# One-hot matrices of a routing built row by row, the order of a kernel's set-up, and attention's maxima as two bf16 halves

## The reference

```python
x = x + moe_top2(layernorm(x), ctx)      # 8 experts, 128 -> 512 -> 128, relu; routed by the context
x = x + moe_top4(layernorm(x))           # 16 experts in 4 groups, the best 2 groups, 4 experts of them
x = x + attention(layernorm(x), ctx)     # 16 heads of 8, mask, softmax, output projection
x = x + 0.5 * mlp(layernorm(x))          # 128 -> 512 -> 128, silu, dequantised weights

# routing of the first layer
scores_topk, idx_topk = jax.lax.top_k(einsum(context, Wg) + bg, 2)
# routing of the second
masked = jnp.where(group_mask[:, :, None], g, -jnp.inf).reshape(T, E)
_, idx = jax.lax.top_k(masked, TOPK)
# softmax of the third
scores = jnp.where(mask, -jnp.inf, einsum('bhsd,bhtd->bhst', qh, kh) * scale)
probs = jax.nn.softmax(scores, axis=-1)
```

## Time and profile before

| | |
|---|---|
| time, median of 3 runs | 1053.17 us (1051.47 to 1054.09) |
| time of the profiled execution | 1050.84 us |
| its span, first to last instruction | 1049.0 us |
| PE busy | 811.3 us (77%) |
| DVE busy | 636.2 us (61%) |
| ACT busy | 500.6 us (48%) |
| POOL busy | 395.2 us (38%) |
| granted TensorE clock, mean | 0.876 of full |

### The profile page before, as it was taken

One profiled execution on the slowest core, in us unless ns is written; L12 is line 12 of the kernel. 1 busy time (PEld: TensorE's weight loads), 2 busy tenths in 40 slices (PEclk: granted clock), 3 DMA queues, 4 the chain that ended last, 5 costly groups with the idle time before them and its releaser, 6 DMA issues.

```text
span 1049.0 us, 17575 instructions
## 1 busy us (share of the span) xinstructions
PE 811.3 (77%) x5374; PEld 621.0 (59%) x5374; DVE 636.2 (61%) x1897; ACT 500.6 (48%) x984; POOL 395.2 (38%) x462
## 2 busy tenths in 40 slices
PE   6577187885789843769877566799789999989898
PEld 4475176764678733657666455688455555555575
DVE  5766053443555812557695344586778888887596
ACT  4443043442465422347644234476255555546586
POOL 5435733005510073443104545410466644446200
PEclk9589678898898965978988868799899999999899
DMA  8482246454311221171021131110344544543011
GB/s 286 132 269 92 87 116 196 164 200 145 103 49 39 71 67 27 42 282 41 23 66 44 53 102 42 57 29 22 105 129 133 139 119 118 165 114 107 5 31 50
DMA packets 96368, 106.54 MB, mean 102 GB/s; under 512 B 12604, under 2 KB 70348, under 8 KB 94999
## 3 DMA queue, kind: packets, MB, share of 16 engines
q1 hardware_dynamic: 76856, 78.04, 23.8%
q0 software_dynamic: 8608, 18.22, 6.8%
q10 hardware_dynamic: 10816, 9.16, 2.8%
HBM read 69.19 MB, written 36.18 MB: 100 GB/s over the span
## 4 chain that ended last, share of the span: by engine, by line
PE 50%; another core or an unknown queue 13%; issue 12%; DVE 11%; ACT 7%; POOL 3%; ACTq 1%; DMA 1%; SPq 1%; DVEq 0%; POOLq 0%
PE y_ps L1872 4%; PE y_ps L2094 3%; PE y_ps L1999 3%; PE hid_ps L1984 3%; PE hid_ps L1860 2%; PE hid_ps L2070 2%; PE hid_ps L2071 2%; PE hid_ps L2082 2%; PE hid_ps L1968 2%; PE tr_ps L2149 2%; PE hid_ps L1850 2%; PE tr_ps L2121 1%; PE hid_ps L1852 1%; PE hid_ps L1969 1%
## 5 line engine op out<-in xcount | busy, mean ns | idle before, releaser
L639 POOL DMA_INDIRECT xr<-b_tokens,idx_sb x70 | 67.0, 957 | 152.6 <-DVE idx_sb L899 105.7
L1121 DVE TENSOR_TENSOR hl<-hid_ps,hh 128x512 fp32r<-128x512 f32 x78 | 53.8, 690 | 110.7 <-ACT hh L1530 73.6
L1872 PE MATMUL y_ps<-region,hh 128*128 x312 | 91.8, 371 | 27.9 <-DVE hl L1121 16.6
L647 POOL DMA_INDIRECT yg<-a_rows,idx_a x64 | 60.9, 952 | 91.8 <-DMA a_rows<-yo 63.3
L1302 DVE TENSOR_REDUCE negmax<-hid_ps 128x4 f32<-128x512 f32 x128 | 85.8, 684 | 8.9 <-PE hid_ps L2071 7.9
L1872 PEld LDWEIGHTS y_ps<-region,hh 128*128 128x128 f32 x312 | 64.8, 208 | 37.0 <-issue 36.6
L1984 PE MATMUL hid_ps<-ident,zb 128*128 128x128 f32 x280 | 49.5, 306 | 45.9 <-DVE hl L1252 24.2
L1860 PE MATMUL hid_ps<-ident,zb 128*128 128x128 f32 x312 | 53.7, 301 | 38.8 <-issue 24.3
L1524 ACT ACTIVATE zb<-hid_ps 128x512 f32<-128x512 f32 x78 | 46.6, 597 | 77.1 <-PE hid_ps L1852 38.8
L1999 PE MATMUL y_ps<-region,hh 128*128 x280 | 82.1, 369 | 0.1
L1241 DVE TENSOR_TENSOR zb<-hid_ps,sg 128x256 f32<-128x256 f32 x70 | 29.7, 424 | 85.5 <-ACT sg L1626 51.3
(11 more groups left out here) (354 smaller groups left out, 2365.1 us busy)
## 6 DMA issues: line engine op xcount, KB each, us to landing
region<-k_strips SPq DMA_DIRECT2D x128, 64.0 KB
region<-k_strips SPq DMA_DIRECT2D x32, 256.0 KB
region<-hl SPq DMA_DIRECT2D x128, 64.0 KB
k_strips<-k_halves SPq DMA_DIRECT2D x24, 256.0 KB
region<-nought SPq DMA_DIRECT2D x6, 1024.0 KB
a_rows<-yo SPq DMA_DIRECT2D x20, 256.0 KB
b_rows<-yo SPq DMA_DIRECT2D x18, 256.0 KB
staged<-a_w_in SPq DMA_DIRECT2D x16, 256.0 KB, 5.8
```

What stands on the lines that cost most here:

```text
L639: g.indirect_dma_start(xr[:, q % 3, j * RB:j * RB + w], None, src, bass.IndirectOffsetOnAxis(ap=rows.bitcast(U32), axis=0)).then_inc(x_got ...
L647: g.indirect_dma_start(yg[:, b % 2, k, j * P:(j + 1) * P], None, ys[h], bass.IndirectOffsetOnAxis(ap=idx[:, h, k, t:t + 1].bitcast(U32), a ...
L1121: v.tensor_tensor(hl[:, n % 2, :], hid_ps[2 + n % 2][:], hh[:, n % 2, :].bitcast(F32), ALU.subtract).then_inc(a_hl, 1)
L1872: t.matmul(y[:, c0:c0 + 2 * P], hh[:, n % 2, cs], w2a[:, bass.ds(e * (2 * FA) + c * 2 * P, 2 * P)], start=c == 0, stop=False)
```

## The change

Three edits.

1. `tile_hots` and `row_hots` make each column of tokens (16 or 2 x 16) in an instruction of its own, tensor_scalar, which compares with a value per partition and, in tile_hots, multiplies with a second one. The operands lohi and idf become fp32; the 0..127 row and the matrices stay fp16.
2. In the set-up ACT copies and rounds only 4 of the 8 folded parts before the tables and the other 4 behind them; PE's prefix sums stand behind the fourth fold instead of the eighth; the wait for the bias row stands behind ACT's first copy.
3. nmpad becomes a bf16 tile at another place of the same memory; DVE writes the high half of the maxima straight into it and the low half by a subtraction that reads it; nm16 and its copy go. PE transposes it with plain bf16 matmuls against a bf16 identity.

```diff
-        id16 = sb("id16", [P, TH], F16)
-        lohi16 = sb("lohi16", [P, 4 * TH], F16)
+        idf = sb("idf", [P, TH])
+        lohi = sb("lohi", [P, 4 * TH])
...
-        nmpad = cpad[:, BT:2 * BT].rearrange("p (b h r) -> p b h r", b=NT, h=HG)
+        nmpad = brows[:, 2 * BT:3 * BT].rearrange("p (b h r) -> p b h r", b=NT, h=HG)
...
             def tile_hots(n, buf):
                 hot = buf[:, 0:2 * TH * n].rearrange("p (k n) -> p k n", k=2 * TH)
-                link(v.tensor_tensor(hot, spread(io16[:], [0, 2 * TH], [1, n]), spread(lohi16[:, 2 * TH:], [1, 2 * TH], [0, n]),
-                                     ALU.is_equal))
-                hot4 = buf[:, 0:2 * TH * n].rearrange("p (k t n) -> p k t n", k=2, t=TH)
-                v.tensor_tensor(hot4, hot4, spread(id16[:], [0, 2], [1, TH], [0, n]), ALU.mult).then_inc(hots, 1)
+                for k in range(2 * TH):
+                    ins = v.tensor_scalar(hot[:, k, :], io16[:, 0:n], lohi[:, 2 * TH + k:2 * TH + k + 1], idf[:, k % TH:k % TH + 1],
+                                          ALU.is_equal, ALU.mult)
+                ins.then_inc(hots, 1)
 
             def row_hots(c, buf):
-                v.tensor_tensor(buf.rearrange("p (k r) -> p k r", r=P), spread(io16[:], [0, TH], [1, P]),
-                                spread(lohi16[:, c * TH:], [1, TH], [0, P]), ALU.is_equal).then_inc(hots, 1)
+                rows = buf.rearrange("p (k r) -> p k r", r=P)
+                for t in range(TH):
+                    ins = v.tensor_scalar(rows[:, t, :], io16[:], lohi[:, c * TH + t:c * TH + t + 1], None, ALU.is_equal)
+                ins.then_inc(hots, 1)
...
-                link(v.tensor_copy(nm16[:, s % 2], negmax[:, s % 2]))
-                v.tensor_copy(nmpad[:, :, :, 3 * HD], nm16[:, s % 2])
-                v.tensor_tensor(nmpad[:, :, :, 3 * HD + 1], negmax[:, s % 2], nm16[:, s % 2], ALU.subtract).then_inc(c_nm, 1)
+                link(v.tensor_copy(nmpad[:, :, :, 3 * HD], negmax[:, s % 2]))
+                v.tensor_tensor(nmpad[:, :, :, 3 * HD + 1], negmax[:, s % 2], nmpad[:, :, :, 3 * HD], ALU.subtract).then_inc(c_nm, 1)
...
-            eng.wait_ge(in_last, 16)
-            for k in range(EA):
+            def unfold(k):
                 eng.wait_ge(fold_mm, k + 1)
                 a.activation(fold_buf(k)[0:P - 1, :], hid_ps[k % 4][0:P - 1, :], ACT.Copy).then_inc(folded, 1)
                 eng.wait_ge(folded, k + 1)
+                if k == 0:
+                    eng.wait_ge(in_last, 16)
                 split_high(k)
+
+            for k in range(EA // 2):
+                unfold(k)
             eng.wait_ge(nb_ready, 1)
             table_a(0)
             table_a(1)
             eng.wait_ge(nb_ready, 2)
             table_a(2)
             table_a(3)
-            for k in range(8, NRAW_A):
+            for k in range(EA // 2, EA):
+                unfold(k)
+            for k in range(EA, NRAW_A):
                 split_high(k)
...
-            for k in range(EA):
+            for k in range(EA // 2):
                 fold(k)
             eng.wait_ge(chosen, 1)
             prefix(EA, 0)
+            for k in range(EA // 2, EA):
+                fold(k)
...
                     for b in range(NT):
-                        ins = t.transpose(tr_ps[:, b * P:(b + 1) * P], nmpad[:, b].rearrange("p h r -> p (h r)"), ident[:])
+                        ins = t.matmul(tr_ps[:, b * P:(b + 1) * P], nmpad[:, b].rearrange("p h r -> p (h r)"), ident16[:],
+                                       start=True, stop=True)
```

More of the change, by code:

```diff
@@ L175, in build @@
         negmax = sb("negmax", [P, 2, NT, HG])
-        nm16 = sb("nm16", [P, 2, NT, HG], BF16)
         rden = sb("rden", [P, NT, HG])
@@ L873, in place_rows @@
                     link(v.tensor_scalar(posi[:, 2], posi[:, 0], 7, None, ALU.logical_shift_right))
-                    v.tensor_copy(lohi16[:, 0:2 * TH], posi[:, 1])
-                    link(v.tensor_copy(lohi16[:, 2 * TH:], posi[:, 2]))
+                    v.tensor_copy(lohi[:, 0:2 * TH], posi[:, 1])
+                    link(v.tensor_copy(lohi[:, 2 * TH:], posi[:, 2]))
             def row_index(h, tmpc, idx):
@@ L982, in _ @@
             v.tensor_copy(bias16[:, 2], biasq[:, 1]).then_inc(bias_split, 1)
-            v.tensor_scalar(id16[:], iotan[:, 0:TH], float(P), rowid, ALU.mult, ALU.add)
+            v.tensor_scalar(idf[:], iotan[:, 0:TH], float(P), rowid, ALU.mult, ALU.add)
             eng.wait_ge(in_x[1], 16)
```

## The result

Measured: 1061.59 us, median of 7 runs (1057.87 to 1064.19), against 1053.77 us (7 runs, 1051.47 to 1058.19). The ratio is 1.0081, 95% interval 1.0055 to 1.0107: 8.5 us slower (5.8 to 11.3). The forecast was 1057.1, 3.9 us slower: the direction came out, the size did not. The profiled execution of the changed kernel took 1060.11 us, with a span of 1058.0.

The account below looks back on a forecast made before the run. Attention was taken to be PE-bound, with PE waiting on DVE's one-hot matrices in the second layer's routing. Set-up +0.4, routings +8.0 and attention -4.5 gave +3.9 us on 1053.17: 1057.1 us, range 1041 to 1063.

Parts of the forecast that it names:

- rival 3: One-hot matrices: one-source instructions stream only two or one element a cycle: 1061.5 (chance 0.08) or 1070 us (0.07).
- the forecast's own bounds: Whole kernel: the forecast by itself, with chance 0.45, gives 1053.5 to 1060.5 us.
- The prices: One-hot matrices: a pointer costs about 0.06 us, 16-bit streaming four a cycle; tile_hots 6.4 us, row_hots 2.5.
- rival 1: One-hot matrices: short instructions run at bare pitch, pointers or not; 1.5 us less a routing, 1041.7 us, chance 0.20.
- rival 2: One-hot matrices: both pointers are fetched together, tile_hots 4.3 us, +2.3 a routing; 1051.7 us, chance 0.15.
- rival 4: Attention: DVE's stall goes and PE waits less; forecast less 7 us, 1050, chance 0.05.
- The path: Second layer's routings: the gather waits for DVE's slot index; 4.0 of 4.3 us count in each, 8.0 us.
- The set-up: Set-up: tile bases lose 2.28 us idle, tables land 4 us earlier, DVE releases first gather about 37.9: +0.4 us.
- the better order pays for the slower matrices: Set-up: the new order's gain nearly offsets the slower one-hot matrices, leaving the set-up 0.4 us later.
- Attention: Attention's maxima: PE saves 0.18 us on 24 steps, DVE's stall stays: -4.5 us, between -1 and -9.
- The sum: Whole kernel: set-up +0.4, second layer +8.0, attention -4.5, together +3.9 us.

Follow-up runs that it names:

- E5: Changed kernel plus extra groups of short and long VectorE instructions in the set-up, writing a scratch area; read from its trace only, no time given.
- E2: Kernel before with only the set-up's new order (folds and tables reordered): ratio 0.9991, -0.9 us.
- E3: Kernel before with only the attention edit (maxima in 16-bit halves, bf16 matmuls): ratio 0.9964, -3.8 us.
- E4: Changed kernel with the old long one-hot matrices restored, so set-up order and attention edit only: ratio 0.9964 against the kernel before, -3.8 us.
- E10: Kernel before with the short instructions of tile_hots only, on another chip: ratio 1.0129, +11.6 us.
- E8: Kernel before with long 16-bit instructions kept, their repeated operand stored twice and read in contiguous pairs: ratio 0.9963, -3.9 us.
- E9: Kernel before with the operand read in pairs, the set-up's new order and the attention edit: ratio 0.9900, 1040.97 us.
- E7: Kernel before with the attention edit's bf16 matmuls only, VectorE keeping its three old instructions: ratio 0.9978, -2.3 us.
- E11: Kernel before with the short instructions of row_hots only, on another chip: ratio 1.0013, +1.2 us.
- E1: Kernel before with only the new short-instruction tile_hots and row_hots (part 1 alone): ratio 1.0152, +16.0 us.
- E12: Kernel before with short tile_hots and row_hots in the second layer's two routings only, on another chip: ratio 1.0094, +8.4 us.
- E6: Kernel before with tile_hots writing its long comparison four times instead of once: ratio 1.0107, +11.3 us.

## Why the prediction came out as it did

**The number.** 1061.6 lies in the range, but 1.1 us above the forecast's own bounds of 1053.5 to 1060.5; the range reached it because it was wide. By the time alone rival 3, with its 1061.5, would look right, and the trace refutes it: its row_hots would run at 0.19 us start to start, and they run at 0.16.

**The prices: right.** Pitch of tile_hots 6.40 / 32 = 0.200 (0.20 forecast), of row_hots 2.59 / 16 = 0.162 (0.158). A pointer costs 0.06, additively (E5), and the 16-bit streaming is near four a cycle: eight fp32 instructions of 128 elements take 0.27 us more than eight in 16 bits, 0.034 each, the difference between 0.067 and 0.033, and 88 elements more cost 0.021 us each in 16 bits (L1010 against L1013), 4.1 a ns. Rivals 1, 2 and 3 are out by L888 and L895 alone, and rival 4 by the 602 ns of L1312: the stall stayed.

**The path: right, and a size too small.** The index of slots does gate the second layer's gathers. The forecast was 4.0 us a routing. The first took 5.2 more (19.7 and 19.6 with short instructions; 14.5, 14.6, 14.6 and 14.4 in the kernel before, E2, E3 and E4) and the second 3.9 to 4.5. VectorE itself is held 3.7 + 0.4 + 0.4 = 4.5 us longer, so in the first 0.7 us come on top, where I had taken 0.3 off for small waits. They stand behind the matrices: TensorE comes back at 1.2 GHz, and VectorE's step at 369.75 waits 1.06 us for ScalarE's copy of TensorE's result, which it does neither in the kernel before nor in E10 (the step in front of it waits 0.4 us less, so 0.7 are left):

```profile
369.75 0.69 DVE L1122 TENSOR_TENSOR hl<-hid_ps,hh 128x512 fp32r<-128x512 f32 x1 [1.06 <-ACT hh L1536]
```

The time at half the clock, added up over stretches of 1 us, goes with the distance from first matrix to gather in all traces but E5's, which wasn't read for it:

| kernels, routing | at 1.2 GHz, us | first matrix to gather, us |
|---|---|---|
| pairs: E8, E9, both routings | 0 | 11.2 to 11.4 |
| long: before, E2, E3, E4, E7, first | 3.4 | 14.4 to 14.6 |
| long: before, second | 3.4 | 14.3 |
| long: E2, E3, E4, E7, second | 6.8 | 14.9 |
| short tile_hots: E10, both | 6.8 | 18.1, 18.0 |
| short row_hots: E11, both | 3.4 | 15.1 |
| all short: changed, E1, E12, second | 6.8 | 18.8 |
| long, four times: E6, second and first | 6.8, 10.3 | 18.5, 19.7 |
| all short: changed, E1, E12, first | 10.2 | 19.3 to 19.7 |

In E10 the hold of 3.7 us costs 3.6 in the first routing, with 6.8 us at half the clock; with 10.2 the 4.5 us cost 5.2.

**The set-up: right in kind, 0.9 us too good, and its gain taken from one trace.** The tile bases start at 22.14, not at 21.35. Two of VectorE's short instructions beside POOL's long run at line 606 take 1.35 (line 936, 0.29 in the kernel before) and 1.15 us (line 953), where the kernel before had one (1.24 at line 952). The new order isn't needed for that: E10, without it, has two as well (1.15 and 1.24), and so has E6 (1.24 and 1.31). The larger point is the 2.28 us of idle time that I counted as gained. Of the other kernels without the new order six have 1.1 to 1.4 us of it (E1, E3, E7, E8, E10, E12), E11 has 2.2 and E6 none. Their tile bases start at 22.36 to 23.13 (E1, E3, E6, E7, E8, on the two slower chips), those of the kernels with it at 22.14 to 22.60 (changed, E2, E4, E9). The means of these, with the kernel before's 23.63, are 22.9 and 22.4: the order brings VectorE about 0.5 us and not 1.5. What it does bring is the tables, 3.9 us earlier where they release the gather (E9; 4.0 forecast). So "the better order pays for the slower matrices" does not hold as it was put: beside them the order is worth 0.25 us (E1 against the changed kernel), and the rest of what seemed to pay for them was one trace of the kernel before, in which the prefix sums start at 22.49 (21.22 to 21.99 in E1, E3, E6, E7 and E8). All of these are single executions.

**Attention: right.** -4.5 forecast, -3.8 by E3 and -4.0 by the stretches above. Where it came from was less right: TensorE saves 0.27 us a step, not 0.18, and gives some of it back as waits for VectorE's maxima, 8.9 us in the changed kernel and 6.0 before (PE's waits from the first of the maxima's transposes on: total, times, longest; the changed kernel, then the kernel before):

```profile
PE hid_ps L2078 <- DVE negmax L1303: 8.9, 10, 3.8
```

```profile
PE hid_ps L2070 <- DVE negmax L1302: 6.0, 7, 3.6
```

**The sum.** With the measured terms it is 1.3 + 5.2 + 4.2 - 4.0 = 6.7 us, inside the interval of 5.8 to 11.3, where 3.9 wasn't. Of the 2.8 us between them the set-up has 0.9, the first routing 1.2, the second 0.2 and attention 0.5. Nearly 2 us of the measured 8.5 stay without a place. Part 1 alone has more of that: +16.0 against 11.2 of its trace, while for E12 8.4 and 9.3 agree. What speaks for the clock: the mean granted clock of its runs is 0.865, that of the kernel before 0.874 on the same chip, of E6 0.869, of the changed kernel 0.870, of E9 0.878; and among 26 runs of the kernel before itself, time and clock go together (correlation -0.83, about 6 us for 0.01). The 6.8 and 3.4 us more at half the clock in the two routings point the same way: an estimate from these rows is that they take at most 5 us of TensorE's work at the full clock, of which only what lies in front of the gather is in the sum above. But a longer wait lowers the clock as much as a lower clock lengthens the time, and no run separated the two. That stays open.

## What to carry to other kernels

A pass that repeats a scalar over a row isn't made cheap by one instruction per row: here each pointer costs 0.06 us, more than 36 to 40 elements take to stream, and 32 instructions with two of them cost 6.4 us where two long ones cost 2.7. Look first at why the long one runs at one element a cycle; storing the repeated value twice and reading it in pairs made it 1.24 us instead of 2.31, with the same instruction count. And price a hold of a helper engine by what stands behind it too: TensorE, left waiting for 4.5 us, came back at half its clock and stayed there for 10.2 us, against 3.4 before. Last, take a gain such as an idle time from more than one trace of the kernel before: this one's 2.28 us were 1.1 to 1.4 in most others.

## What the runs showed of the hardware that was not expected

- Two-source instructions with 16-bit elements run at two elements a cycle if all operands, the repeated one too, are read in contiguous pairs: 2048 elements in 1.24 us each (L1025 of E5). The Trainium skill's page "VectorE: DVE Perf Modes", section "The perf-mode tier table", gives 1224 ns for such an instruction in 16 bits and 2293 at one element a cycle; the rows agree with both (1.24 and 2.31 us). I had read the old instructions' one a cycle as a property of the operation.
- The same program takes 15% less time on another chip. The kernel before takes 898.0 us there (17 runs; 896.5 in one run on the chip of E5) and 1053.3 on the chip of E6 to E9; the mean granted clock was 0.932 against 0.873. The difference lies in the first two layers: attention, from the first to the last transposes of the maxima, takes 221.8 us in E11 and 224.9 in the kernel before, but begins at 589.1 there and at 737.9 here. ScalarE's waits between 40 and 300 us differ most: on the first chip its activation at line 1524 alone waits 19.8 us for something "remote" and its others 19.5, 14.9 and 14.4 (rows below, kernel before: total, times, longest); in E10, E11 and E12 on the second no wait in that stretch is put down to it. What it waits for isn't in the profile, and no run here looked for it.

```profile
ACT zb L1524 <- remote: 19.8, 4, 7.9
ACT yo L1539 <- remote: 19.5, 3, 12.0
```

- Runs of one kernel on one chip spread by 1% (1046.3 to 1058.7 for the kernel before), so the parts of this change, 1 to 4 us each, had to be read from distances inside the trace, such as first matrix to gather, which repeat within 0.2 us for the first routing and 0.6 for the second. The 0.6 go with the clock: 14.3 us with 3.4 of them at 1.2 GHz, 14.9 with 6.8.
